# Gated cross attention and a block-sparse feed forward on one core: the feed forward's transposes leave TensorE

## The chip, the cores and the metric

One core of a Trainium2 chip runs the whole kernel. The metric is the device time of one launch in microseconds. Lower is better. Three runs of the kernel before gave 1849.33, 1851.08 and 1852.5 us; their median is 1851.08 us.

## What is computed

The reference is one layer: cross attention with a gate, then a feed forward that keeps one inner value of each block of 32, also with a gate. Both are preceded by a layer norm.

```python
x = x + tanh(g_xattn[0]) * xattn(layernorm(x), ctx, mask, bias, Wq, Wk, Wv, Wo)   # x: (32, 64, 512), 32 heads of 128
x = x + tanh(g_ffn[0]) * ffn(layernorm(x), c1_w, c2_w, w1, w2t)

def ffn(x):                                   # xf: (2048, 512) rows
    inter = xf @ c1_w.T @ c2_w.T              # rank 16, then 1792 inner values
    blk = inter.reshape(B * T, 56, 32)
    idx = argmax(blk, axis=-1) + arange(0, 1792, 32)   # the first largest of each block
    h = relu(einsum('bkm,bm->bk', w1[idx], xf))
    return einsum('bk,bkm->bm', h, w2t[idx])
```

The kernel doesn't gather rows. It computes all 1792 values of `xf @ w1.T`, multiplies them by a mask that is one at the first largest of each block, and multiplies the result by `w2t`. Everything is in fp32. A large product is made of three matmuls on a high and a low part of each operand (`three`, L1487 to L1490).

## The kernel before

The 2048 rows are 16 tiles of 128 rows (`PAIRS`). There are three stages. The first projects q, k and v and stores them in device memory. The second is attention: 128 slots (`SLOTS`, 16 groups of heads by 8 tiles), taken in 64 pairs (`DUOS`, loop variable `d`). The third is the feed forward over the 16 tiles. No scheduler places anything: each engine's program is written out, and semaphores join them. The order in a queue is the order of the code, and an instruction that waits holds everything behind it on its engine. This holds for SyncE as well, which issues all DMAs of these stages.

Per tile `t` the feed forward does this:

- VectorE norms the tile (`f_stats`, `f_norm`; GpSimd makes the reciprocal root in `do_rstd`), TensorE turns it by four transposes (`f_transpose_x`), ScalarE copies the high part (`fx_hi`) and VectorE takes the low part (`fx_lo`).
- TensorE `low_rank(u)` makes the rank-16 product for two tiles at once (12 matmuls of 256 columns), VectorE `low_rank` splits it, and TensorE `selector(t, k)` makes the 1792 selector values in four pieces.
- ScalarE copies these (`sel`), VectorE takes the maximum of each block (`block_max`) and marks the equal ones (`mark_max`, tile `is_max`), GpSimd multiplies the marks by a falling weight (`rank`), and VectorE finds the first (`block_rank`, `first_max`).
- TensorE `hidden(t, k)` makes `xf @ w1.T` in pieces of 512, 512, 512 and 256 columns, 12 matmuls each. VectorE `pick_h` takes the relu and the mask (tile `h_picked`).
- TensorE turns `h_picked` by 14 transposes (`transpose_h`), ScalarE copies the high part (`ht_hi`), VectorE takes the low part (`ht_lo`), TensorE makes 42 matmuls of 512 columns (`output`), and VectorE adds the gated result to the tile (`finish`). SyncE stores it.

In the main loop, iteration `j` on TensorE holds `output(j - 1)`, the transposes of `h_picked` of tile j between its pieces, and `hidden(j + 1)` with `selector(j + 2)` piece by piece. VectorE's iteration `j` holds the low parts of tile j, `block_rank`, `first_max` and `pick_h` of tile j + 1, and `block_max` and `mark_max` of tile j + 2. The weights w1 and w2 are split during attention into high and low parts, stored in device memory, and loaded back from slot 120 on (`load_w1`, `load_w2`, seven pieces of 1 MB each). PSUM has eight banks; `ffn_uses` lists which use of the feed forward has which bank, and `bank_free` gives the semaphore that frees it.

## Time and profile before

| | us |
|---|---|
| median of three runs | 1851.08 |
| the profiled execution | 1849.7 |
| its span, first to last instruction | 1847.5 |
| TensorE busy in the span | 1833.6 (99%) |
| VectorE, ScalarE, GpSimd busy | 1089.4, 686.3, 955.5 |
| share of the end chain on TensorE | 79% |

The span is the time between the first and the last instruction of one execution. Busy time of TensorE counts overlapping matmuls once. A matmul row of 512 columns has a duration of 0.39 us, but the next one starts 0.23 us after it, so the step between starts is what a matmul costs here. In the rows below, "idle before" is the idle time of an engine just ahead of a group, with the instruction that ended it. The projections take until about 940 us, attention until about 1482 us, and the feed forward the rest.

### The profile page before, as it was taken

To read this page: it belongs to the slowest core of one execution; us is meant where nothing else is said; L and a number is where in the kernel's file an instruction comes from. 1 tells how busy PE (TensorE), PEld (TensorE's weight loads), DVE (VectorE), ACT (ScalarE), POOL (GpSimd) and SP (SyncE) were. 2 spreads that over 40 slices of the span, in tenths; PEclk is the share of its full clock that TensorE was granted. 3 is DMA by queue.
4 is the path that set the end of the run, shared out by engine and by line. 5 is a ranking of instruction groups with operands and counts; after the bars stand their busy time and mean duration, and the time that the engine had idled before them with its cause. 6 is when DMAs were issued, how large, how long until landed. Compare 5 with 4: busy or idle time off the path is not lost.

```text
span 1847.5 us, 37822 instructions
## 1 busy us (share of the span) xinstructions
PE 1833.6 (99%) x15260; PEld 1580.0 (86%) x15260; DVE 1089.4 (59%) x1774; ACT 686.3 (37%) x1761; POOL 955.5 (52%) x758
## 2 busy tenths in 40 slices
PE   9999999999999999999999999999999999999999
PEld 7899988899998888888878888888888888888887
DVE  5444467433346465333457676786676887777673
ACT  4322233322233233333346556555555422222221
POOL 5767688766668888778735334333333121111110
PEclk9999999999999999999999999999999999999999
DMA  5555566644455554467658878798787650000000
GB/s 183 198 173 185 192 203 201 211 143 161 142 188 189 183 186 165 165 219 244 230 206 359 339 277 319 301 377 347 274 328 292 249 200 25 26 25 23 24 12 18
DMA packets 131293, 359.51 MB, mean 195 GB/s; under 512 B 12080, under 2 KB 53424, under 8 KB 120624
## 3 DMA queue, kind: packets, MB, share of 16 engines
q1 hardware_dynamic: 131120, 357.09, 53.9%
q8 instruction: 122, 2.00, 0.4%
q14 instruction: 51, 0.42, 0.1%
HBM read 229.11 MB, written 127.93 MB: 193 GB/s over the span
## 4 chain that ended last, share of the span: by engine, by line
PE 79%; DVE 2%; DMA 1%; ACT 1%; issue 1%; POOL 0%; DVEq 0%; SPq 0%; ACTq 0%
PE bank L1488 23%; PE bank L1490 22%; PE bank L1489 22%; PE bank L1589 3%; PE bank L1553 3%; PE bank L1569 2%; PE bank L1702 1%; PE bank L1679 1%; DMA x_tile<-in_x 1%; ACT scores L891 0%; PE bank L1658 0%; DMA ln_x<-in_x 0%; DVE attn_sum L1296 0%; DVE attn_t_lo L1268 0%; POOL wv_s_lo L751 0%
## 5 line engine op out<-in xcount | busy, mean ns | idle before, releaser
L1488 PE MATMUL bank<-tokens_hi,wkq_hi 128*128 128x512 f32 x888 | 346.8, 391 | 1.5 <-DVE tokens_lo L1063 0.8
L1489 PE MATMUL bank<-tokens_lo,wkq_hi 128*128 128x512 f32 x888 | 345.7, 389 | 0.0
L1490 PE MATMUL bank<-tokens_hi,wkq_lo 128*128 128x512 f32 x888 | 345.5, 389 | 0.0
L751 POOL TENSOR_TENSOR wkq_lo<-raw_wkq,wkq_hi 128x768 fp32r<-128x768 f32 x126 | 278.6, 2232 | 122.3 <-ACT wkq_hi L856 122.3
L1488 PE MATMUL bank<-wv_s_hi,tokens_hi 128*128 128x256 f32 x896 | 253.8, 283 | 1.5 <-POOL wv_s_lo L751 1.5
L1490 PE MATMUL bank<-wv_s_hi,tokens_lo 128*128 128x256 f32 x896 | 253.6, 283 | 0.0
L1489 PE MATMUL bank<-wv_s_lo,tokens_hi 128*128 128x256 f32 x896 | 253.6, 283 | 0.0
L1488 PE MATMUL bank<-wo_hi,attn_t_hi 128*128 128x512 f32 x512 | 205.7, 402 | 1.2 <-DVE attn_t_lo L1268 1.2
L1488 PEld LDWEIGHTS bank<-tokens_hi,wkq_hi 128*128 128x128 f32 x888 | 166.7, 188 | 39.3 <-DVE c L1113 3.0
L1490 PE MATMUL bank<-wo_hi,attn_t_lo 128*128 128x512 f32 x512 | 199.8, 390 | 0.0
L1489 PE MATMUL bank<-wo_lo,attn_t_hi 128*128 128x512 f32 x512 | 199.3, 389 | 0.0
L1490 PEld LDWEIGHTS bank<-tokens_hi,wkq_lo 128*128 128x128 f32 x888 | 166.7, 188 | 34.8
L1489 PEld LDWEIGHTS bank<-tokens_lo,wkq_hi 128*128 128x128 f32 x888 | 166.8, 188 | 33.8
L891 ACT ACTIVATE scores<-scores,negmax 128x64 f32<-128x64 f32 x512 | 172.2, 337 | 44.7 <-DVE negmax L1178 44.7
L880 ACT ACTIVATE p<-bank 128x512 f32<-128x512 f32 x94 | 56.2, 598 | 334.2 <-PE bank L1490 334.2
L751 POOL TENSOR_TENSOR wv_s_lo<-raw_wv,wv_s_hi 128x1536 fp32r<-128x1536 f32 (+1 forms) x32 | 130.1, 4065 | 96.1 <-ACT wv_s_hi L856 96.1
L1091 DVE TENSOR_TENSOR c<-bank,u 128x512 f32<-128x512 f32 x94 | 65.0, 692 | 188.2 <-PE bank L1490 188.2
L1488 PEld LDWEIGHTS bank<-wv_s_hi,tokens_hi 128*128 128x128 f32 x896 | 172.0, 192 | 2.5 <-POOL wv_s_lo L751 2.4
L1489 PEld LDWEIGHTS bank<-wv_s_lo,tokens_hi 128*128 128x128 f32 x896 | 172.0, 192 | 0.2
L1490 PEld LDWEIGHTS bank<-wv_s_hi,tokens_lo 128*128 128x128 f32 x896 | 172.0, 192 | 0.0
L779 POOL TENSOR_TENSOR wo_lo<-raw,wo_hi 128x1024 fp32r<-128x1024 f32 x30 | 71.6, 2388 | 158.0 <-DVE wo_hi L1255 158.0
L1113 DVE TENSOR_TENSOR c<-bank,u 128x512 f32<-128x512 f32 x94 | 64.7, 688 | 148.1 <-PE bank L1490 148.0
(148 smaller groups left out, 3688.4 us busy)
## 6 DMA issues: line engine op xcount, KB each, us to landing
k_t<-c SPq DMA_DIRECT2D x128, 256.0 KB, 2.4
v_by_token<-c SPq DMA_DIRECT2D x128, 256.0 KB, 2.3
q_t<-c SPq DMA_DIRECT2D x128, 256.0 KB, 2.3
kt<-k_t SPq DMA_DIRECT2D x16, 2048.0 KB, 9.7
qt<-q_t SPq DMA_DIRECT2D x16, 2048.0 KB, 14.2
v<-v_by_token SPq DMA_DIRECT2D x16, 2048.0 KB, 12.8
raw_wkq<-in_wk SPq DMA_DIRECT2D x32, 512.0 KB, 4.1
raw_wv<-in_wv SPq DMA_DIRECT2D x16, 1024.0 KB, 5.4
```

Of the source, the lines that this page charges most:

```text
L751: pool.tensor_tensor(lo, job_raw(r)[:, a:b, :], hi.bitcast(F32), ALU.subtract)\
L779: pool.tensor_tensor(lo, raw[n % 2][:, 0:cols], hi.bitcast(F32), ALU.subtract)\
L880: act.activation(e1[n % 2][:, :], bank[n % 2][:, :], ACT.Copy).then_inc(act_e1, 1)
L891: e = act.activation(sc[s % 2][:, h, :], sc[s % 2][:, h, :], ACT.Exp, bias=negmax[s % 2][:, h:h + 1], scale=1.0, accum_out=rsum[s % 2][:, ...
L1091: dve.tensor_tensor(o_c["c12"][n % 2][:, :], bank[5 + n % 2][:, :], u2[:, :], ALU.add)\
L1113: dve.tensor_tensor(o_c["c22"][n % 2][:, :], bank[5 + n % 2][:, :], u3[:, :], ALU.add)\
L1488: pe.matmul(o, a[0], b[0], start=first_mm, stop=False, skip_group_check=not grouped)
L1489: pe.matmul(o, a[0], b[1], start=False, stop=False, skip_group_check=not grouped)
L1490: return pe.matmul(o, a[1], b[0], start=False, stop=last_mm, skip_group_check=not grouped)
L1553: mm = pe.matmul(bank[SCORE_BANK[r % 2]][h * S:(h + 1) * S, o:o + S], qt[it % 2][:, 2 * r_ + h, cols], kt[it % 2][:, 2 * r_ + h, cols], st ...
L1569: mm = pe.transpose(bank[PT_BANK[d % 2]][:, o:o + P], sc[a][:, 2 * r:2 * r + 2, :].rearrange("p h k -> p (h k)"), ident[:, :])
L1589: mm = pe.matmul(bank[PV_BANK[b]][dims, o:o + S], v[it % 2][keys, p, h, dims], pt[keys, s % 2, h, :], start=True, stop=True)
```

## The change

The transposes of the feed forward leave TensorE. VectorE turns a tile in blocks of 32 by 32 (`transpose` in `f_norm` and in the new `turn_h`), the result is stored to device memory, and loaded back so that the rows of each block land where the full transpose needs them (`store_xf`, `load_xf`, `store_h`, `load_h` on SyncE). The order of the inner dimension in c1, w1 and w2 is permuted to suit (`by_block`). ScalarE reads the high parts from SBUF, and GpSimd takes over both low parts (`fx_lo`, `ht_lo`) from VectorE. `h_picked` is turned in two halves, of 1024 and of 768 columns (`HALF`).

The rank-16 product holds high and low parts of c1 in one stationary tile, so it is 8 matmuls of 256 columns and not 12. `hidden` and the selectors run one tile further ahead: iteration `j` has `output(j - 1)`, `hidden(j + 2)` and `selector(j + 3)`. Six tiles (`X_EARLY`) are normed and turned in attention, one per pair of slots from d = 56 on, where before two were normed at d = 60 and two at its end. w2's fourth piece is asked for in attention, and its pieces 5 and 6 ahead of 4. The tiles have nine buffers (`X2R`), and the arena grows from 207 to 222 KB.

```diff
 def ffn_uses():
...
+    sel, hid = (2, 3), (4, 5, 1, 6, 0)
...
@@ sync @@
+            def store_xf(t):
+                sp.wait_ge(dve_xb, t + 1)
+                sp.dma_start(xf_d[t], fxb[t % 2][:, :]).then_inc(xf_out[t % 2], 16)
+            def load_xf(t):
+                sp.wait_ge(xf_out[t % 2], 16 * (t // 2 + 1))
...
+            def store_h(t, i):
+                sp.wait_ge(dve_hb, 2 * t + i + 1)
+                sp.dma_start(h_d[i][t], hmb[i][:, :]).then_inc(h_out[i], 16)
+            def load_h(t, i):
+                sp.wait_ge(h_out[i], 16 * (t + 1))
+                if t:
+                    sp.wait_ge(pool_hl, 4 * (t - 1) + 2 * i + 2)
+                sp.dma_start(hraw[i][:, :, :], h_d[i][t].rearrange("(q g) (r f) -> (g r) q f", q=4, r=4))\
+                    .then_inc(h_in[i], 16)
...
@@ gpsimd @@
+            def ht_lo(t, g):
+                pool.wait_ge(act_h, 4 * t + g + 1)
+                pool.tensor_tensor(hmt_part(g, 1), hraw_part(g), hmt_part(g, 0).bitcast(F32), ALU.subtract)\
+                    .then_inc(pool_hl, 1)
...
+            for j in range(-1, PAIRS):
+                if j >= 0:
+                    for g in range(4):
+                        ht_lo(j, g)
+                if j % 2 == 0 and j + 7 < PAIRS:
+                    do_rstd(LN + j + 6)
+                    do_rstd(LN + j + 7)
+                if j + 3 < PAIRS:
+                    rank(j + 3)
+                if j % 2 and j + 6 < PAIRS:
+                    fx_lo(j + 5)
+                    fx_lo(j + 6)
@@ vector @@
+                    dve.transpose(fxb[t % 2][:, :], fxn[:, :]).then_inc(dve_xb, 1)
...
+            def turn_h(t, i):
+                a, w = HALF[i]
+                dve.wait_ge(dve_hm, 4 * t + 2 * i + 2)
+                if t:
+                    dve.wait_ge(h_out[i], 16 * t)
...
+                dve.transpose(hmb[i][:, :], hm[:, a:a + w]).then_inc(dve_hb, 1)
...
+            for j in range(-1, PAIRS + 1):
+                if j < 0:
+                    low_rank(1)
+                if j % 2 and 0 < j and j + 6 < PAIRS:
+                    f_norm((j + 5, j + 6))
+                if j + 2 < PAIRS:
+                    block_rank(j + 2)
+                    first_max(j + 2)
+                if j > 0:
+                    finish(j - 1)
+                if j % 2 and 0 < j and j + 3 < PAIRS:
+                    low_rank((j + 3) // 2)
+                for k in range(4):
+                    if j + 2 < PAIRS:
+                        pick_h(j + 2, k)
+                        if k % 2:
+                            turn_h(j + 2, k // 2)
+                    if j + 3 < PAIRS:
+                        block_max(j + 3, k)
+                    if k == 2 and j % 2 == 0 and j + 7 < PAIRS:
+                        f_stats((j + 6, j + 7))
+                if j + 3 < PAIRS:
+                    mark_max(j + 3)
@@ tensor @@
-            def f_transpose_x(t):
...
-            def transpose_h(t, k):
...
+            for j in range(1, PAIRS + 1):
                 for k in range(4):
                     output(j - 1, k)
+                    if j == 1:
+                        selector(3, k)
+                if j % 2 and j + 3 < PAIRS:
+                    low_rank((j + 3) // 2)
                 for k in range(4):
+                    if j + 2 < PAIRS:
+                        hidden(j + 2, k)
+                    if j + 3 < PAIRS:
+                        selector(j + 3, k)
```

GpSimd at the start of the feed forward, before: the marks of two tiles (`rank(0)`, `rank(1)`) after the statistics of tiles 2 and 3, and then more of the same (`is_max` is the tile of marks).

```order
L762 TENSOR_TENSOR ln_rstd_61<-ln_var_eps_59,minus_half 128x1 [waits pool_own]
L784 TENSOR_TENSOR is_max<-is_max,earlier_is_larger 128x1792 [waits dve_ffn_ismax] x2
L758 TENSOR_SCALAR ln_var_eps_58<-ln_mean_var_56 128x1 [waits dve_xn,dve_stat]
L762 TENSOR_TENSOR ln_rstd_60<-ln_var_eps_58,minus_half 128x1 [waits pool_own]
L758 TENSOR_SCALAR ln_var_eps_59<-ln_mean_var_57 128x1 [waits dve_xn,dve_stat]
```

GpSimd at the same place, now (the `xft_lo` rows are `fx_lo`, the `h_picked_t_lo` rows `ht_lo` of tile 0).

```order
L880 TENSOR_TENSOR is_max<-is_max,earlier_is_larger 128x1792 [waits dve_ffn_ismax]
L870 TENSOR_TENSOR xft_lo<-raw_xft_184,xft_hi 128x4x128 [waits act_ffn_xt_hi]
L870 TENSOR_TENSOR xft_lo<-raw_xft_185,xft_hi 128x4x128 [waits act_ffn_xt_hi]
L880 TENSOR_TENSOR is_max<-is_max,earlier_is_larger 128x1792 [waits dve_ffn_ismax] x2
L870 TENSOR_TENSOR xft_lo<-raw_xft_184,xft_hi 128x4x128 [waits act_ffn_xt_hi]
L870 TENSOR_TENSOR xft_lo<-raw_xft_185,xft_hi 128x4x128 [waits act_ffn_xt_hi]
L875 TENSOR_TENSOR h_picked_t_lo<-raw_h_t_188,h_picked_t_hi 128x512 [waits act_ffn_ht_hi] x2
L875 TENSOR_TENSOR h_picked_t_lo<-raw_h_t_189,h_picked_t_hi 128x512 [waits act_ffn_ht_hi]
```

The low parts of tile 0, which `output(0)` needs, stand on GpSimd behind the marks of tiles 1 and 2 and the low parts of x of tiles 4 and 5.

VectorE before, from `mark_max(3)` at the end of iteration 1 to the split of the rank-16 product of tiles 4 and 5 in iteration 2.

```order
L1347 TENSOR_TENSOR is_max<-selector,block_max 128x1792 [waits dve_ffn_first,dve_step]
L1377 TENSOR_TENSOR h_picked_t_lo<-bank,h_picked_t_hi 128x512 [waits act_ffn_ht_hi] x2
L1316 TENSOR_TENSOR xft_lo<-bank,xft_hi 128x4x128 [waits act_ffn_xt_hi] x2
L1352 TENSOR_REDUCE block_first<-is_max 128x56 [waits pool_ffn_rank]
L1377 TENSOR_TENSOR h_picked_t_lo<-bank,h_picked_t_hi 128x512 [waits act_ffn_ht_hi]
L1358 TENSOR_TENSOR first_max_155<-is_max,block_first 128x1792 [waits dve_ffn_hm,dve_step]
L1377 TENSOR_TENSOR h_picked_t_lo<-bank,h_picked_t_hi 128x256 [waits act_ffn_ht_hi]
L1328 CAST low_rank_stacked_182<-bank 128x256 [waits pe_ffn_inter,pe_ffn_t]
L1330 TENSOR_TENSOR low_rank_stacked_182<-bank,low_rank_stacked_182 64x256 [waits dve_step]
```

VectorE now, from `mark_max(3)` to the same split for tiles 4 and 5 (iteration 1).

```order
L1448 TENSOR_TENSOR is_max<-selector,block_max 128x1792 [waits dve_ffn_first,dve_step]
L1181 TENSOR_SCALAR xn<-x_tile_178,ln_mean_var_56,ln_rstd_60 128x512 [waits pool_rstd,dve_ffn_xn_by_block]
L1420 STREAM_TRANSPOSE xn_by_block_182<-xn 128x512 [waits dma_ffn_xn_by_block0,dve_xn]
L1181 TENSOR_SCALAR xn<-x_tile_179,ln_mean_var_57,ln_rstd_61 128x512 [waits pool_rstd,dve_ffn_xn_by_block]
L1420 STREAM_TRANSPOSE xn_by_block_183<-xn 128x512 [waits dma_ffn_xn_by_block1,dve_xn]
L1453 TENSOR_REDUCE block_first<-is_max 128x56 [waits pool_ffn_rank]
L1459 TENSOR_TENSOR first_max_155<-is_max,block_first 128x1792 [waits dve_ffn_hm,dve_step]
L1486 SCALAR_TENSOR_TENSOR x_tile_172<-bank,gate_tanh,x_tile_172 128x512 [waits pe_ffn_out]
L1429 CAST low_rank_stacked_192<-bank 128x256 [waits pe_ffn_inter,pe_ffn_t]
L1431 TENSOR_TENSOR low_rank_stacked_192<-bank,low_rank_stacked_192 64x256 [waits dve_step]
```

The split of the rank-16 product now stands behind the marks of tile 3, GpSimd's work on them, the two operations that find the first, and the finish of tile 0.

TensorE before, where the rank-16 product of tiles 4 and 5 begins (behind the transposes of `h_picked` of tile 2; the selectors of tile 3 were done one iteration earlier).

```order
L1702 MATMUL bank<-ident,h_picked 128x128 [waits dve_ffn_hm,dve_ffn_xt_lo]
L1702 MATMUL bank<-ident,h_picked 128x128
L1488 MATMUL bank<-xft_hi,c_hi 128x256 [waits dve_ffn_xt_lo]
L1489 MATMUL bank<-xft_lo,c_hi 128x256
L1490 MATMUL bank<-xft_hi,c_lo 128x256
```

TensorE now, from the last selector piece of tile 3 to the first matmuls of `hidden(3, 0)`; `selector(4, 0)`, which waits for the split (`dve_ffn_t`), comes 12 matmuls after the first of these.

```order
L1757 MATMUL bank<-c_stacked,low_rank_stacked_193 128x256 [waits dve_ffn_t,act_ffn_inter]
L1746 MATMUL bank<-xft_hi,c_stacked 128x256 [waits pool_ffn_xt_lo,act_ffn_inter]
L1746 MATMUL bank<-xft_hi,c_stacked 128x256 x3
L1746 MATMUL bank<-xft_lo,c_stacked 128x256 x4
L1573 MATMUL bank<-w_hi,xft_hi 128x512 [waits pool_ffn_xt_lo,dve_ffn_hm]
```

So between the selector piece of tile 3 that VectorE's marks need and the selector piece of tile 4 that needs VectorE's split there are 8 matmuls of 256 columns and 12 of 512.

## Rows read from the trace of the kernel before

**Rows 1.** The page, part 1: busy time, share of the span, instructions.
```profile
PE 1833.6 (99%) x15260; PEld 1580.0 (86%) x15260; DVE 1089.4 (59%) x1774; ACT 686.3 (37%) x1761; POOL 955.5 (52%) x758
```

**Rows 2.** Waits of TensorE from 1440 us to the end: total, times, longest.
```profile
PE bank L1488 <- DVE h_picked L1368: 0.7, 1, 0.7
```

**Rows 3.** TensorE in order of time: start, duration, instruction, feed forward.
```profile
1622.40 0.39 PE L1489 MATMUL bank<-w_lo,h_picked_t_hi 128*128 128x512 f32 x1
...
1622.86 0.60 PE L1702 MATMUL bank<-ident,h_picked 128*128 128x128 f32 x4
1623.21 0.47 PE L1488 MATMUL bank<-w_hi,h_picked_t_hi 128*128 128x512 f32 x1
1623.52 0.39 PE L1489 MATMUL bank<-w_lo,h_picked_t_hi 128*128 128x512 f32 x1
...
1626.48 1.18 PE L1658 MATMUL bank<-ident,xn 128*128 128x128 f32 x8
1627.41 0.47 PE L1488 MATMUL bank<-w_hi,h_picked_t_hi 128*128 128x512 f32 x1
...
1632.06 0.38 PE L1702 MATMUL bank<-ident,h_picked 128*128 128x128 f32 x2
1632.19 0.36 PE L1488 MATMUL bank<-xft_hi,c_hi 128*128 128x256 f32 x1
...
1633.70 0.40 PE L1488 MATMUL bank<-w_hi,xft_hi 128*128 128x512 f32 x1
...
1646.88 0.60 PE L1702 MATMUL bank<-ident,h_picked 128*128 128x128 f32 x4
```

**Rows 4.** TensorE in order of time, end of attention.
```profile
1481.91 1.03 PE L1658 MATMUL bank<-ident,xn 128*128 128x128 f32 x8
```

**Rows 5.** VectorE groups, 1550 to 1750 us: busy, mean ns, idle before.
```profile
L1347 DVE TENSOR_TENSOR is_max<-selector,block_max 128x1792 bf16<-128x1792 f32 x9 | 18.2, 2026 | 0.3
L1358 DVE TENSOR_TENSOR first_max<-is_max,block_first 128x1792 bf16<-128x1792 bf16 x9 | 18.1, 2015 | 0.0
L1368 DVE SCALAR_TENSOR_TENSOR h_picked<-bank,first_max 128x512 f32<-128x512 f32 x26 | 18.0, 692 | 23.8 <-PE bank L1490 23.1
L1070 DVE BATCH_NORM_STATS2 ln_stats<-x_tile 128x6 f32<-128x512 f32 x8 | 5.5, 689 | 0.0
L1330 DVE TENSOR_TENSOR low_rank_stacked<-bank,low_rank_stacked 64x256 fp32r<-64x256 f32 x4 | 1.7, 428 | 0.1
```

**Rows 6.** VectorE groups of the whole span, one form each.
```profile
L1083 DVE STREAM_TRANSPOSE ln_xn_by_block<-ln_xn 128x512 f32<-128x512 f32 x16 | 11.2, 701 | 0.0
L1076 DVE TENSOR_SCALAR xn<-x_tile,ln_mean_var,ln_rstd 128x512 f32<-128x512 f32 x16 | 8.6, 545 | 4.5 <-POOL ln_rstd L762 4.5
L1063 DVE TENSOR_TENSOR tokens_lo<-raw_tokens,tokens_hi 128x1024 fp32r<-128x1024 f32 x19 | 32.2, 1693 | 7.0 <-ACT tokens_hi L873 7.0
L1063 DVE TENSOR_TENSOR tokens_lo<-raw_tokens_first,tokens_hi 128x1024 fp32r<-128x1024 f32 x3 | 3.7, 1221 | 0.4 <-ACT tokens_hi L873 0.4
```

**Rows 7.** VectorE in order of time, first tiles of the feed forward.
```profile
1490.73 2.03 DVE L1347 TENSOR_TENSOR is_max<-selector,block_max 128x1792 bf16<-128x1792 f32 x1
1492.67 2.21 DVE L1368 SCALAR_TENSOR_TENSOR h_picked<-bank,first_max 128x512 f32<-128x512 f32 x4
```

**Rows 8.** GpSimd in order of time.
```profile
1452.70 1.27 POOL L779 TENSOR_TENSOR c_lo<-raw,c_hi 128x512 fp32r<-128x512 f32 x1 [12.34 <-ACT c_hi L955]
1492.84 3.60 POOL L784 TENSOR_TENSOR is_max<-is_max,earlier_is_larger 128x1792 bf16<-128x1792 bf16 x1 [8.60 <-DVE is_max L1347]
```

**Rows 9.** Start of the kernel, windows of 1 us: length, TensorE busy (instructions), clock, DMA.
```profile
3.00:4.00 1.00, 1.00 (x6) 1.00 1.02 381
5.00:6.00 1.00, 1.00 (x9) 1.00 0.84 279
7.00:8.00 1.00, 1.00 (x12) 1.00 0.93 328
```

**Rows 10.** DMA issues, 1525 to 1840 us: count, size, us to landing.
```profile
out<-x_tile SPq DMA_DIRECT2D x14, 256.0 KB, 2.0
```

More of the change, by code:

```diff
@@ L92, in ffn_uses @@
 def ffn_uses():
[L94 to L118 removed]
+    used = {}
@@ new lines, in next_of @@
+    def next_of(banks, use):
+        k = used.get(banks, 0)
+        used[banks] = k + 1
+        return (use, banks[k % len(banks)])
+    sel, hid = (2, 3), (4, 5, 1, 6, 0)
+    out = [(("t", 0), 0), (("sel", 0, 0), 7), (("sel", 0, 1), 0)]
+    out += [next_of(sel, ("sel", 0, k)) for k in (2, 3)]
+    out += [next_of(sel, ("sel", 1, k)) for k in (0, 1)]
+    out += [next_of(hid, ("h", 0, k)) for k in (0, 1)]
+    out += [next_of(sel, ("sel", 1, k)) for k in (2, 3)]
+    out += [next_of(hid, ("h", 0, k)) for k in (2, 3)]
@@ new lines, in ffn_uses @@
+    out.append(next_of(sel, ("t", 1)))
+    out += [next_of(hid, ("h", 1, 0)), (("h", 1, 1), 7), next_of(sel, ("sel", 2, 0))]
+    for k in (2, 3):
+        out += [next_of(hid, ("h", 1, k)), next_of(sel, ("sel", 2, k - 1))]
+    out += [next_of(hid, ("h", 2, 0)), next_of(sel, ("sel", 2, 3))]
+    out += [next_of(hid, ("h", 2, k)) for k in (1, 2, 3)]
+    for j in range(1, PAIRS + 1):
+        out.append(next_of(hid, ("out", j - 1)) if j == PAIRS - 1 else (("out", j - 1), 7))
+        if j == 1:
+            out += [next_of(sel, ("sel", 3, k)) for k in range(4)]
+        if j % 2 and j + 3 < PAIRS:
+            out.append(next_of(sel, ("t", (j + 3) // 2)))
+        for k in range(4):
@@ L688, in _ @@
                         load_w1(n)
-                if s == SLOTS - 6:
-                    load_x2(3)
+                for t in range(X_EARLY):
+                    if s == SLOTS - 22 + 2 * t:
+                        load_x2(t)
+                    if s == SLOTS - 14 + 2 * t:
+                        store_xf(t)
+                    if t < 4 and s == SLOTS - 11 + t + t // 2 * 5:
+                        load_xf(t)
                 if it % G == G - 1 and it < ITERS:
@@ L697, in _ @@
                     sp.wait_ge(kept_out, 32 * KEPT)
[L698 to L710 removed]
+                for n in {0: (0,), 1: (1, 2, 3)}.get(s - SLOTS, ()):
+                    load_w2(n)
+            load_w2(5)
+            load_w2(6)
+            load_w2(4)
+            load_xf(4)
+            load_xf(5)
+            store_h(0, 0)
+            for j in range(-1, PAIRS + 1):
+                ahead = j % 2 and 0 < j and j + 6 < PAIRS
+                if j + 1 < PAIRS:
+                    store_h(j + 1, 1)
+                if ahead:
+                    store_xf(j + 5)
+                    store_xf(j + 6)
+                if j < 0:
+                    load_h(0, 0)
+                    load_h(0, 1)
+                    load_x2(6)
+                    load_x2(7)
+                    load_x2(8)
+                if X2R <= j + 7 < PAIRS:
+                    load_x2(j + 7)
+                if 0 <= j < PAIRS - 1:
+                    load_h(j + 1, 0)
+                if ahead:
+                    load_xf(j + 5)
+                    load_xf(j + 6)
+                if 0 <= j < PAIRS - 1:
+                    load_h(j + 1, 1)
+                if j > 0:
+                    sp.wait_ge(dve_o, j)
+                    sp.dma_start(out[j - 1], x2[(j - 1) % X2R][:, :]).then_inc(out_sem[(j - 1) % X2R], 16)
+                if j + 2 < PAIRS:
+                    store_h(j + 2, 0)
             for k in range(X2R):
@@ L830, in _ @@
                         do_lo(n)
-            for j in range(PAIRS):
-                if j % 2 and j + 4 < PAIRS:
-                    do_rstd(LN + j + 3)
-                    do_rstd(LN + j + 4)
-                if j + 2 < PAIRS:
-                    rank(j + 2)
+            for j in range(-1, PAIRS):
[10 more added lines that the diff above has]
+                    fx_lo(j + 6)
         @block.scalar
```

334 lines of the change are left out of this document (137 added, 197 removed).

## The prediction

> **What bounds the kernel now.** I read the page's busy times first: TensorE is busy for 99% of the span, no other engine for more than 59% [rows 1]. Then the waits of TensorE from the end of attention on: one, of 0.7 us [rows 2]. So the feed forward is TensorE's own queue, end to end, and an instruction taken out of it is worth its step as long as nothing becomes late. Third, TensorE in order of time, for the steps [rows 3]: from 1622.40 to 1622.86 there are two steps, so matmuls of 512 columns start 0.23 us apart, whatever their listed duration of 0.39.
>
> **What leaves TensorE.** Four transposes take from 1622.86 to 1623.21, and the matmul behind them takes a step of 0.31 instead of 0.23: 0.43 us. Two take 0.13 and cost the next matmul 0.09: 0.22. A tile has three groups of four and one of two, 1.51 us; 16 tiles give 24.2. Eight transposes of x, from 1626.48 to 1627.41, with the longer step behind them, are 1.01 for two tiles, 8.1 for all. The rank-16 product, 12 matmuls from 1632.19 to 1633.70, has a step of 0.12, and loses four of them eight times: 3.8. Sum: **36.1 us less** on TensorE [rows 3]. Its iteration was 24.0 us with such a product in it (1622.86 to 1646.88); it becomes 21.1, and 20.1 without.
>
> **What VectorE and GpSimd get.** VectorE loses both low parts (about 3 us a tile) and gains transposes: 0.70 for 512 columns [rows 6], so by length about 1.2 and 0.9 for the halves. Listed durations of neighbours overlap: four picks take 2.21 together [rows 7]. A tile costs it 2.2 for the picks, 2.2 for the block maxima, which are as long, 2.03 + 2.0 + 2.0 for marks and first, 0.75 for the finish (one PSUM and one SBUF input like a pick), 2.1 for the halves, and on average 2.6 for norm, turn, statistics and split [rows 5, 6]: 15.9 of 20.6 us. GpSimd: 3.6 for the marks, a low part of 512 columns at 1.27 [rows 8], four pieces of h 4.5, x 1.3: about 10. Nobody is full. The trips through memory (a store lands in 2.0 us [rows 10]; I give a load 2.5) have two iterations of room in the steady loop. The cost is in the order of the queues, at three places.
>
> **Before output(0).** Attention's matmuls ended at 1481.9 [rows 4]; without the x transposes and four matmuls ahead of it, at about 1480.4. From there TensorE has hidden of three tiles (9.6 each), the selectors and one rank-16 product, 30.9 us, and wants output(0) at 1511.4. That needs the low part of h, which GpSimd makes behind rank(2) and two low parts of x. The chain to it: mark_max(1) began at 1490.73 [rows 7], and begins 1.2 earlier, since GpSimd's first marks follow TensorE: done 1491.5. VectorE then picks and turns tile 0 (4.4), splits (0.85), finds the first of tile 1 (4.0), picks and turns tile 1 with tile 2's maxima (6.9), and marks tile 2 (2.0): 1509.6. GpSimd: marks 3.6, x twice 2.5, h 1.3: 1517.2 with the gaps between engines [rows 5, 8]. **A wait of 5.7 us.** The trips of h hide behind this chain: the store can go at 1496, has 3 MB of w2 ahead of it, 8 us at the 381 GB/s of a full queue [rows 9], and with its own 2.0 and the load's 2.5 the data are there at 1508.5, 7 us ahead of need. Another wait I take at selector(0): TensorE comes 1.5 earlier by what was removed ahead of it, VectorE's split does not have to. Bounds 0 and 1.5, value 0.8.
>
> **In iteration 1.** The selectors of tile 3 are placed between the pieces of output(0), so they end with it, and not at the end of an iteration. Behind them TensorE has 1.0 of rank-16 and 2.7 of hidden(3, 0), and then selector(4, 0), which waits for VectorE's split of tiles 4 and 5. VectorE gets to it by way of the last copies and picks of tile 2 and its turn, which lag 3.1 (the statistics of two tiles, 1.75, stand there), mark_max(3) 2.0, GpSimd's marks 3.7, block_rank and first_max 4.0, finish 0.75, split 0.9, and gaps: about 14.7 after the selectors, against 3.7 [rows 3, 5, 8]. **A wait of 11.0 us.** It happens once; afterwards selectors end with the iteration.
>
> **In the odd iterations 3, 5, 7, 9.** Counted from the iteration's start, VectorE marks by 5.2 (it had two statistics in the even one), GpSimd by 8.9 (the norms and turns of two tiles, 2.6, run meanwhile), first found 13.0, finish 13.7, split 14.7. TensorE is at that selector at 13.3. **1.4 us each, 5.6.** In 11 and 13 there are no norms, and no wait by this count. For the even ones no split is waited for.
>
> **The clock after a wait.** TensorE never waits over 2.4 us in this trace, so no row shows what a wait of 5 or 11 us does. The start of the kernel is the nearest: the same matmul is done 6 times in a microsecond at 3 us, 9 times at 5 us and 12 times at 7 us [rows 9], so for about 3 us the rate is that of the lower level, 1.2 GHz and not 2.4, a loss of 1.5 us, though the granted clock in the rows reads 1.00 there. Bounds: 0, and 1.5 at each of the two long waits and each of the four short ones, 9. I take two, 3.1, since the long ones are nearest to a start.
> The Trainium skill (TensorE: Matmul & The Clock Gate, "Loop structure matters more than you think") says that a long wait between matmuls drops TensorE to the low clock. The half rate at the start agrees with its rule for an idle engine; no run here shows it in the middle. By it the sum has the 3.1, without it 3.1 less.
>
> **Two engines in SBUF.** A VectorE subtraction with two SBUF inputs took 1.22 us where GpSimd was quiet and 1.69 among GpSimd's work [rows 6]. Now GpSimd works while VectorE is in first_max. Bounds: 0, and 0.8 at each of the five waits that first_max is part of, 4.0. I take a third, 1.4, because GpSimd is busy in the feed forward for half of the time only.
> The Trainium skill (GPSIMD Engine Reference, "Specifications") has the rule: GpSimd shares its SBUF interfaces with VectorE, with contention where VectorE reads two SBUF inputs or runs in a two-port mode. The two rows agree, and the rule speaks against this change: by it the sum has the whole 4.0.
>
> **In attention** VectorE gets 2.0 us more per pair of slots from d = 55 to 61. It idles for 41% of the span [rows 1], and the new work stands at the end of its turns, ahead of a step that waits for TensorE; I take nothing, and 2 us as the other bound. The same goes for SyncE, whose new stores wait for the turns: the weights behind them come up to 4 us later, and the last piece of w1 is not asked for later than before.
>
> **Sum.** −36.1 + 5.7 + 0.8 + 11.0 + 5.6 + 3.1 + 1.4 = −8.5. The profiled execution took 1849.7 us (span 1847.5 and 2.2 around it), so 1841.2; the median shown is 1.4 above it, so **1842.6**.
>
> **Rivals.**
> 1. The waits at output(0) and selector(4, 0) come, but neither a clock loss nor contention, and the odd iterations just fit: −36.1 + 17.5 = −18.6, so 1832.5. For it: 1.4 of 13.3 us is little, and VectorE's steps overlap by 0.09. Against: the rows at the start and the pair of subtractions.
> 2. Nothing waits: the whole 36.1, 1815. It would need GpSimd's marks off the way to output(0), and the order rows say they are on it.
> 3. Slower: VectorE and GpSimd hold the loop. Each tile has 15.9 of VectorE and, in the even iterations with nothing to fill it, 3.7 of waiting for GpSimd's marks: 19.6, against 20.6 of TensorE on average. If the factor of the two subtractions, 1.69/1.22, holds for the marks, for first_max and for GpSimd's marks in every tile, that is 0.8 + 0.8 + 1.4 = 3.0 more, 22.6, and TensorE waits 2.0 in each of 13 iterations: 26.0. They take the place of the 5.6 and 1.4: −8.5 − 7.0 + 26.0 = +10.5, so 1861.6. It decides from 20.6 us of chain per tile. For it: the pair of rows. Against: marks and first_max run while GpSimd mostly waits for VectorE.
> 4. The trips of h are late at the start, where the queue is full: if the data come at 1521 instead of 1508.5, output(0) waits 5 us longer: −3.5, so 1847.6. For it: 7 MB of w2 and the last stores of x stand in the same queue. Against: 7 us of room.
>
> **Chances.** Forecast 0.50 (its own range 1836 to 1848), rival 1 0.28, rival 2 0.05, rival 3 0.09, rival 4 0.08. Against the median, 0.2% is 3.7 us, about what a measurement of this kernel can tell from no change. Below 1847.4: all of 1 and 2, nine tenths of the forecast and a third of rival 4: 0.81. Within: 0.10. Slower: 0.09. The range leaves out rival 2 and most of 3: 1829 to 1851.
>
> **What would show it.** In the trace of the changed kernel: TensorE waits once, 5 to 6 us, for GpSimd's h_picked_t_lo near 1511; once, about 11, for VectorE's split behind the selectors of tile 3; and a little over 1 us four times for the same split. TensorE's busy time falls by some 36 us. The matmuls behind the two long waits start 0.45 us apart for about 3 us. VectorE's first_max stays between 2.0 and 2.8. If the first long wait is for a DMA, rival 4 holds; if TensorE waits in every iteration, rival 3; if iteration 1 has no wait, my reading of the queues is wrong.

## The result, and the profile after

The changed kernel takes 1860.6 us (median of 4 runs, 1858.7 to 1863.4), the kernel before 1851.0 beside it (1849.3 to 1852.5): ratio 1.0054, 95% interval 1.0036 to 1.0071. It is slower by half a per cent; I had said 1842.6 and faster. The profiled execution took 1858.7 (span 1856.9), 17.5 us more than the 1841.2 that my sum gave for it.

The page of the changed kernel, busy times and TensorE's granted clock over 40 slices of the span:

```profile
PE 1803.4 (97%) x14940; PEld 1552.0 (84%) x14940; DVE 1102.8 (59%) x1742; ACT 688.2 (37%) x1761; POOL 1073.3 (58%) x838
...
PEclk9999999999999999999999999999999988999999
```

TensorE is busy for 30.2 us less than before [rows 1], with 320 matmuls fewer, and yet the span grew by 9.4. So it now stands still for 39.6 us that it did not before, and two slices show less than the full clock. Of the 39.6 us, 38.8 are in the waits of the next two lines, so the tiles that are normed and turned in attention cost TensorE next to nothing there. Waits of TensorE from 1380 us to the end (total, times, longest), where before there was one of 0.7 [rows 2]:

```profile
PE bank L1757 <- DVE low_rank_stacked L1431: 28.8, 7, 12.8
PE bank L1573 <- DVE h_picked L1469: 10.7, 1, 10.7
```

The same in order of time, the instruction that each wait of over 1 us ends with (start, duration, instruction, idle time before; three more of 3.33 or 3.34 follow at 1645.89, 1690.36 and 1734.81):

```profile
1468.59 1.05 PE L1757 MATMUL bank<-c_stacked,low_rank_stacked 128*128 128x512 f32 x4 [1.41 <-DVE low_rank_stacked L1431]
...
1499.87 0.47 PE L1757 MATMUL bank<-c_stacked,low_rank_stacked 128*128 128x512 f32 x1 [1.20 <-DVE low_rank_stacked L1431]
...
1525.46 0.76 PE L1573 MATMUL bank<-w_hi,h_picked_t_hi 128*128 128x512 f32 x1 [10.73 <-DVE h_picked L1469]
...
1555.41 0.77 PE L1757 MATMUL bank<-c_stacked,low_rank_stacked 128*128 128x512 f32 x1 [12.82 <-DVE low_rank_stacked L1431]
...
1601.43 0.47 PE L1757 MATMUL bank<-c_stacked,low_rank_stacked 128*128 128x512 f32 x1 [3.33 <-DVE low_rank_stacked L1431]
```

The places are those that the prediction named: output(0), the first selector behind those of tile 3, and the selectors of the odd iterations. The sizes are not. The releaser named at 1525.46 is misleading: VectorE's pick there has nothing to do with output(0); what output(0) needs is GpSimd's first low part of h, which ends at 1525.36. First wait, GpSimd; the third row holds all four low parts, the fourth row the first of them alone, and VectorE's first_max stands beside it:

```profile
1516.36 3.56 POOL L880 TENSOR_TENSOR is_max<-is_max,earlier_is_larger 128x1792 bf16<-128x1792 bf16 x1 [18.10 <-DVE is_max L1448]
1519.88 2.48 POOL L870 TENSOR_TENSOR xft_lo<-raw_xft,xft_hi 128x512 fp32r<-128x512 f32 x2
1522.32 6.18 POOL L875 TENSOR_TENSOR h_picked_t_lo<-raw_h_t,h_picked_t_hi 128x512 fp32r<-128x512 f32 x4
...
1522.32 3.04 POOL L875 TENSOR_TENSOR h_picked_t_lo<-raw_h_t,h_picked_t_hi 128x512 fp32r<-128x512 f32 x1
```

```profile
1522.01 2.23 DVE L1459 TENSOR_TENSOR first_max<-is_max,block_first 128x1792 bf16<-128x1792 bf16 x1
```

Marks, two low parts of x, then h: the order that the prediction had, but the marks begin at 1516.36, not 1509.6. Why is in VectorE's row of the same stretch, and in SyncE's DMA issues:

```profile
1509.57 1.25 DVE L1482 STREAM_TRANSPOSE h_by_block<-h_picked 128x1024 f32<-128x1024 f32 x1 [3.76 <-DMA h_by_block<-h_by_block]
```

```profile
1498.52 0.32 SPq L613 DMA_DIRECT2D w_hi<-w_hi_lo  x1
1498.89 0.43 SPq L613 DMA_DIRECT2D w_lo<-w_hi_lo  x1
1499.42 0.92 SPq L646 DMA_DIRECT2D raw_xft<-ffn_xn_by_block  x2
1500.40 2.52 SPq L651 DMA_DIRECT2D h_by_block<-h_by_block  x2
1509.49 1.31 SPq L657 DMA_DIRECT2D raw_h_t<-h_by_block  x2
```

VectorE's turn of tile 1 writes the buffer out of which tile 0 is stored. The store is issued at 1500.40 behind w2; SyncE's load, which waits for it to land, goes at 1509.49, and VectorE, which waits for the same, at 1509.57, after 3.76 us. The third wait is VectorE's queue in iteration 1:

```profile
1542.17 2.02 DVE L1448 TENSOR_TENSOR is_max<-selector,block_max 128x1792 bf16<-128x1792 f32 x1
1544.12 0.54 DVE L1181 TENSOR_SCALAR xn<-x_tile,ln_mean_var,ln_rstd 128x512 f32<-128x512 f32 x1
1544.69 0.71 DVE L1420 STREAM_TRANSPOSE xn_by_block<-xn 128x512 f32<-128x512 f32 x1
1545.44 2.93 DVE L1181 TENSOR_SCALAR xn<-x_tile,ln_mean_var,ln_rstd 128x512 f32<-128x512 f32 x1
1548.40 0.71 DVE L1420 STREAM_TRANSPOSE xn_by_block<-xn 128x512 f32<-128x512 f32 x1
1549.03 1.98 DVE L1453 TENSOR_REDUCE block_first<-is_max 128x56 bf16<-128x1792 bf16 x1
1551.04 2.76 DVE L1459 TENSOR_TENSOR first_max<-is_max,block_first 128x1792 bf16<-128x1792 bf16 x1
1553.73 0.74 DVE L1486 SCALAR_TENSOR_TENSOR x_tile<-bank,gate_tanh,x_tile 128x512 f32<-128x512 f32 x1
1554.39 0.41 DVE L1429 CAST low_rank_stacked<-bank 128x256 fp32r<-128x256 f32 x1
```

with GpSimd's marks beside it:

```profile
1544.28 3.80 POOL L880 TENSOR_TENSOR is_max<-is_max,earlier_is_larger 128x1792 bf16<-128x1792 bf16 x1 [2.86 <-DVE is_max L1448]
```

The same norm takes 0.54 and then 2.93 us. The long one ends at 1548.37, and GpSimd's marks at 1548.08. This repeats in each odd iteration up to 9, ten norms in all (count, then busy, mean ns, idle before):

```profile
L1181 DVE TENSOR_SCALAR xn<-x_tile,ln_mean_var,ln_rstd 128x512 f32<-128x512 f32 x10 | 17.5, 1754 | 0.2
```

Their mean of 1.75 is against 0.55 before [rows 6]. And first_max takes 2.76, against 2.02 [rows 5].

Last, the clock behind the waits. Windows of 1 us: length, TensorE busy (instructions), clock, DMA share and GB/s:

```profile
1526.00:1527.00 1.00, 1.00 (x4) 0.50 0.00 0
1530.00:1531.00 1.00, 1.00 (x4) 0.50 0.72 167
1532.00:1533.00 1.00, 1.00 (x6) 1.00 0.00 1
1556.00:1557.00 1.00, 1.00 (x4) 0.50 0.73 182
1560.00:1561.00 1.00, 1.00 (x6) 1.00 0.00 0
1737.00:1738.00 1.00, 1.00 (x4) 0.50 0.51 195
```

Granted clock 0.50 is the lower level, 1.2 GHz, and matmuls start 0.43 us apart, not 0.23: 14 of them from 1525.46 (2.9 us lost), 8 from 1555.41 (1.65), about 7 near 1736 to 1739, behind a wait of 3.33 (1.5).

### The profile page after: what moved, and what is told of

Its sections match the earlier page's. It is cut to its first block, busy times and chain, and to the rows that moved or that the text cites. A ratio compares the mean times of both kernels' runs of the same rounds, so it can differ in the third digit from the quotient of the medians.

```text
span 1856.9 us, 37340 instructions
## 1 busy us (share of the span) xinstructions
PE 1803.4 (97%) x14940; PEld 1552.0 (84%) x14940; DVE 1102.8 (59%) x1742; ACT 688.2 (37%) x1761; POOL 1073.3 (58%) x838
## 4 chain that ended last, share of the span: by engine, by line
PE 70%; DVE 6%; issue 4%; POOL 1%; DMA 1%; ACT 1%; DVEq 0%; ACTq 0%; POOLq 0%
PE bank L1573 21%; PE bank L1575 20%; PE bank L1574 20%; PE bank L1674 3%; PE bank L1638 3%; PE bank L1654 2%; DVE xn L1181 1%; DMA x_tile<-in_x 1%; DVE block_first L1453 1%; POOL is_max L880 1%; PE bank L1757 1%; DVE attn_sum L1401 1%; ACT scores L996 1%; DVE ln_stats L1175 0%; DVE is_max L1448 0%
## 5 line engine op out<-in xcount | busy, mean ns | idle before, releaser
L1573 PEld LDWEIGHTS bank<-tokens_hi,wkq_hi 128*128 128x128 f32 x888 | 166.7, 188 | 38.8 <-DVE c L1218 3.0
```

What stands on the lines that cost most here:

```text
L1573: pe.matmul(o, a[0], b[0], start=first_mm, stop=False, skip_group_check=not grouped)
```

## The experiments

All are edits of the changed kernel, timed in 3 to 5 rounds beside the kernel before, whose median in these calls was 1850.3, 1850.4 and 1850.0. They ask which wait each step of a queue makes, what the long norm is, and what the half rate is worth.

**1. GpSimd's order at the start** (lo_first).

```
+            for g in range(4):
+                ht_lo(0, g)
             for j in range(-1, PAIRS):
-                if j >= 0:
+                if j >= 1:
                     for g in range(4):
                         ht_lo(j, g)
```

> The changed kernel with one edit: GpSimd makes the low parts of h of tile 0 ahead of the marks of tile 2 and the low parts of x of tiles 4 and 5. Theory (the order of GpSimd's queue holds output(0)): ScalarE has the high part of h at 1513.9, so the first low part is done near 1515.3 and TensorE's wait of 10.73 us there falls to under 1 us, its half-rate stretch with it. The marks of tile 2 start some 2 us later (4.5 us of h from 1513.9 against 1516.36), first_max(2) ends near 1526.4, and from there VectorE has 11 us of its own work up to the end of mark_max(3): 1537.4 instead of 1544.2. The split of tiles 4 and 5 comes 6.8 earlier, while TensorE is there 13 us earlier: its wait of 12.8 grows to about 19, and the whole kernel gains 6.8: about 1854. Rival (the wait is for the DMA, h itself late): the 10.73 stays at 8 or more and the time within 2 us of 1860.6. Second rival (the second wait is VectorE work that moves along with TensorE): gain 13, 1848.

Measured: 1857.1 us (1853.3 to 1859.6), ratio 1.0036 (1.0024 to 1.0049). TensorE at output(0) and behind the selectors of tile 3, and GpSimd:

```profile
1517.79 0.47 PE L1575 MATMUL bank<-w_hi,h_picked_t_hi 128*128 128x512 f32 x1 [1.61 <-issue]
...
1552.20 0.76 PE L1759 MATMUL bank<-c_stacked,low_rank_stacked 128*128 128x512 f32 x1 [19.39 <-DVE low_rank_stacked L1433]
```

```profile
1516.42 6.24 POOL L875 TENSOR_TENSOR h_picked_t_lo<-raw_h_t,h_picked_t_hi 128x512 fp32r<-128x512 f32 x4 [16.70 <-ACT h_picked_t_hi L1086]
1522.62 3.61 POOL L880 TENSOR_TENSOR is_max<-is_max,earlier_is_larger 128x1792 bf16<-128x1792 bf16 x1
```

The first wait goes from 10.73 to 1.61, so nearly all of it was GpSimd's order and not the data; the next grows from 12.8 to 19.4, as expected (19). The two waits are one chain through VectorE: the first gives 9.1 and the second takes 6.6 of it back. The gain is 3.5 and not 6.8, because the four low parts took 6.2 us and began at 1516.42, so GpSimd's marks came 4 us later than expected; the half rate stands behind two of the four waits of 3.33.

**2. VectorE's split earlier** (split_first).

```
+                if j == 1:
+                    low_rank(2)
                 if j % 2 and 0 < j and j + 6 < PAIRS:
                     f_norm((j + 5, j + 6))
                 if j + 2 < PAIRS:
                     block_rank(j + 2)
+                if j % 2 and 1 < j and j + 3 < PAIRS:
+                    low_rank((j + 3) // 2)
+                if j + 2 < PAIRS:
                     first_max(j + 2)
                 if j > 0:
                     finish(j - 1)
-                if j % 2 and 0 < j and j + 3 < PAIRS:
-                    low_rank((j + 3) // 2)
```

> The changed kernel with one edit: VectorE splits the rank-16 product of tiles 4 and 5 ahead of the norms of iteration 1, and in the iterations 3, 5, 7, 9 right behind block_rank, ahead of first_max and finish. Theory (TensorE waits for the split's place in VectorE's queue): the wait of 12.8 falls by the 10.2 us between the end of mark_max(3) and the split's old start, to 2.6; the four of 3.33 lose first_max 2.7 and finish 0.7 and vanish; the half-rate stretches behind them (1.65 and 1.5 us) go too. Sum 10.2 + 13.3 + 3.1 = 26.6: about 1834. Rival (VectorE and GpSimd hold the loop with what contention adds): the waits come back for picks or low parts of h further on, and the gain is less than half: 1848 or more.

Measured: **1834.5 us** (1833.6 to 1835.6), ratio 0.9914 (0.990 to 0.9927). Moving two VectorE instructions, the split, turns the change from slower to faster. TensorE: the wait is 2.56 (2.6 expected), one of 2.34 for finish(0) is new, and of the four of 3.33 one of 1.75 is left. Windows of 50 us of the same kernel:

```profile
1600.00:1650.00 50.00, 50.00 (x238) 1.00 0.41 129
1650.00:1700.00 50.00, 50.00 (x243) 1.00 0.42 133
```

From 1600 on TensorE does not wait, though the norms of the odd iterations still take 2.97 there. So VectorE and GpSimd do not hold the loop, contention and all; rival 3 of the prediction is out, and that its time, 1861.6, was nearest is luck.

**3. The first trip of h ahead of w2** (h_first).

```
-            load_w2(5)
-            load_w2(6)
-            load_w2(4)
             load_xf(4)
-            load_xf(5)
             store_h(0, 0)
+            load_xf(5)
...
                     load_h(0, 1)
+                    load_w2(5)
+                    load_w2(6)
+                    load_w2(4)
```

> The changed kernel with one edit: SyncE issues the first store of h and both loads of it ahead of the last three pieces of w2. Theory (the first trip of h waits in the DMA queue behind 3 MB of w2): VectorE's wait of 3.76 us for the block buffer goes, the marks of tile 2 start near 1512.6 instead of 1516.36, TensorE's wait of 10.73 falls to 7.0, and everything behind moves along: about 1857. Rival (the trip is as long whatever stands ahead of it): no change, 1860.6. Second rival (now w2 is late): TensorE waits for a DMA in output(0), and the gain is lost.

Measured: 1858.9 us (1857.0 to 1859.7), ratio 1.0044 (1.0031 to 1.0056). The turn of tile 1 no longer waits (it starts at 1506.62), and the wait at output(0) is 7.03, as expected:

```profile
1522.53 0.77 PE L1573 MATMUL bank<-w_hi,h_picked_t_hi 128*128 128x512 f32 x1 [7.03 <-DVE h_picked L1469]
```

Of the 3.7 only 1.7 show in the time. In the profiled execution the half rate now stands behind three of the four waits of 3.33, where in the changed kernel it was one; at some 1.5 us each that is the missing 2 and more.

**4. Unused matmuls in the waits** (filler: the two long ones; fill_all: the four of 3.33 too). `fill(o, n)` issues n matmuls of 512 columns into the bank that is used next, and nothing reads what they leave.

```
+                if t in (4, 6, 8, 10, 12) and k == 0:
+                    fill(bank[f_bank[("sel", t, k)]], 54 if t == 4 else 13)
                 pe.wait_ge(dve_ft, u + 1)
...
+                if t == 0 and k == 0:
+                    fill(bank[f_bank[("out", t)]], 45)
                 pe.wait_ge(pool_hl, 4 * t + k + 1)
```

> The changed kernel with matmuls whose results are not used added in the two long waits of TensorE: 45 of 512 columns (10.3 us at 0.23) ahead of output(0), 54 (12.4 us) ahead of the first selector of tile 4. Theory (the half rate comes from the idleness): the granted clock stays at 1.00, the matmuls behind both places start 0.23 us apart at once, which is worth 2.9 + 1.65 us: about 1856. Rival (the clock drops for another reason, or the fillers push the chain): no gain or slower, 1860.6 or more.

> The kernel with the unused matmuls of the filler run, and 13 more of 512 columns (3.0 us) in each of the four waits of 3.33 ahead of the first selectors of tiles 6, 8, 10 and 12. Theory (any wait of 3 us or more can bring the half rate, and in the filler run it came behind short waits in place of the long ones): the granted clock is 1.00 throughout the feed forward, all six half-rate microseconds of the changed kernel (2.9 + 1.65 + 1.5) are gone, about 1854.6. Rival (the half rate comes at times of its own, whatever TensorE does): stretches under 1.00 stay, and the time is that of the filler run, 1857.6, or more.

Measured: filler 1857.6 us (1855.0 to 1861.5), ratio 1.0040 (1.0027 to 1.0052); fill_all 1853.0 (1851.5 to 1854.7, 11 runs), ratio 1.0016 (1.0007 to 1.0025). In filler the clock behind both long waits is 1.00, but all four waits of 3.33, of which one had it in the changed kernel, now have the half rate behind them, as here:

```profile
1598.79 0.77 PE L1763 MATMUL bank<-c_stacked,low_rank_stacked 128*128 128x512 f32 x1 [3.32 <-DVE low_rank_stacked L1431]
```

In fill_all no window in which TensorE works is below 1.00, and the kernel is 7.6 us faster (7.0 by the two ratios) with 151 matmuls more and the same chain on VectorE:

```profile
1599.00:1600.00 1.00, 1.00 (x6) 1.00 0.30 110
1736.00:1737.00 1.00, 1.00 (x11) 1.00 0.98 401
```

So the half rate comes from TensorE's idleness, and cost 6 to 8 us here: 6.1 by the steps, 7.6 by this run.

**5. What the long norm is** (norm_apart, dve_rank, quarters). Three edits: the norms moved out of the marks' time; the ranks made on VectorE; GpSimd's marks in four instructions.

```
norm_apart:
+                if j % 2 == 0 and 0 <= j and j + 7 < PAIRS:
+                    f_norm((j + 6, j + 7))
                 if j + 3 < PAIRS:
                     mark_max(j + 3)
dve_rank (block_rank, ahead of its reduce; rank(t) leaves GpSimd):
-                dve.wait_ge(pool_e, t + 1)
+                dve.wait_ge(dve_e, t + 1)
+                after(link(dve.tensor_tensor(is_max[:, :, :], is_max[:, :, :],
+                    rank_w[:, :].unsqueeze(1).broadcast_to([P, NBLK, SPARSITY]), ALU.mult)))
quarters (rank(t) on GpSimd):
+                for q in range(4):
+                    part = is_max[:, 14 * q:14 * (q + 1), :]
```

> The changed kernel with one edit: VectorE norms and turns the two coming tiles at the end of the even iteration, ahead of mark_max, instead of at the start of the odd one, where GpSimd makes its marks. Theory (VectorE's norm and GpSimd's marks get in each other's way): every norm takes 0.55 us, none 2.9. The chain to the split gets 2.6 longer by the moved work and 1.1 shorter behind it (from the end of mark_max to block_rank 3.75 instead of 4.83), so the waits of 12.8 and 3.33 become about 14 and 4.8 and the time rises by some 7 us, 1868. Rival (the second norm is long by its own form or by its place behind a transpose): it stays at 2.9 where it is now.

> The changed kernel with one edit: the product of is_max with the ranks is made by VectorE ahead of block_rank and not by GpSimd; nothing else moves. Theory (contention with GpSimd's marks): the norms take 0.55 us each and first_max 2.03, since GpSimd is idle or at small work beside them. From the end of mark_max to the split: norms and turns 2.5, ranks 2.0, block_rank 2.0, first_max 2.0, finish and split 1.6, 10.1 us instead of 11.2, so the waits of 12.8 and 3.33 become 11.7 and 2.2, five times 1.1: about 1855. Rival (VectorE's 2.0 us more per tile hold the loop): TensorE waits in even iterations too, and the kernel is slower than 1861. Second rival (no contention, the long norm is its own): the norm stays at 2.9 and the waits at 3.3 or more.

> The changed kernel with one edit: GpSimd makes the ranks of a tile in four instructions of 448 columns instead of one of 1792. Theory (VectorE's norm and an instruction of GpSimd exclude each other: the norm runs when the one on GpSimd has ended): the second norm of an odd iteration, 2.9 us beside one instruction, ends behind the quarter that it meets, in 1.5 us or less, while GpSimd's marks take 3.7 plus at most 1 in all; block_rank starts when they end. The waits of 3.33 fall by 0.8 at most if the quarters cost nothing, and rise by as much as the four cost more: 1858 to 1862. Rival (both slow down by sharing, whatever the length of GpSimd's instruction): the second norm stays near 2.9.

Measured, the norms of the feed forward in norm_apart, dve_rank and quarters, each group's columns being busy, mean ns and idle before:

```profile
L1181 DVE TENSOR_SCALAR xn<-x_tile,ln_mean_var,ln_rstd 128x512 f32<-128x512 f32 x10 | 5.4, 540 | 0.2
```

```profile
L1175 DVE TENSOR_SCALAR xn<-x_tile,ln_mean_var,ln_rstd 128x512 f32<-128x512 f32 x10 | 10.8, 1079 | 0.2
```

```profile
L1182 DVE TENSOR_SCALAR xn<-x_tile,ln_mean_var,ln_rstd 128x512 f32<-128x512 f32 x10 | 9.7, 970 | 0.2
```

norm_apart: all norms at 0.54, so the 2.9 is GpSimd's work beside them and nothing in the norm. Time 1871.8 (1870.2 to 1873.7), ratio 1.0111 (1.0095 to 1.0127), above the 1868 expected: the waits are 13.55 and 4.02, near the 14 and 4.8 expected, but the half rate stands behind every one of them, mean clock 0.984. quarters: 1857.1 (1855.8 to 1857.7), ratio 1.0039 (1.0024 to 1.0053); the second norm and the quarters:

```profile
1546.35 1.38 DVE L1182 TENSOR_SCALAR xn<-x_tile,ln_mean_var,ln_rstd 128x512 f32<-128x512 f32 x1
```

```profile
1545.19 4.41 POOL L882 TENSOR_TENSOR is_max<-is_max,earlier_is_larger 128x448 bf16<-128x448 bf16 x4 [2.85 <-DVE is_max L1449]
```

A shorter instruction on GpSimd makes a shorter norm on VectorE, 1.38 for 2.93. So says exclusion, by which an instruction ends only behind the one that it met on the other engine; sharing, by which both are slow for as long as they overlap, does not. The waits fall from 12.82 to 12.02 and from 3.33 to about 2.5. That is the 0.8 which I had given if the quarters cost nothing, but they cost 0.6 (4.41 for 3.80), and the time is just below my 1858 to 1862. Only 0.3 comes from the norm, since block_rank starts 4.5 us after mark_max and not 4.8; the rest is first_max, 2.23 for 2.76, which met less of a low part of h, and that I had not foreseen.

dve_rank: 1845.5 us (1844.2 to 1848.2), ratio 0.9974 (0.9963 to 0.9985), 10 better than I expected. I had forgotten that this edit too takes the marks from in front of h on GpSimd: at output(0) TensorE does not wait (first matmul at 1515.23), and the next waits are 14.2 and 2.30. The norm is 1.5 us at the first of a pair and 0.6 at the second: GpSimd is then at its low parts of h. The ranks cost VectorE 1.05 us where GpSimd is quiet, against 3.56 to 3.80 for GpSimd in the changed kernel.

**6. Together** (best: edits 1 and 3, the split of tiles 4 and 5 and finish(0) in iteration 0, later splits behind block_rank; best_dve_rank: and the ranks on VectorE; best2: and this).

```
+                if j == 2:
+                    finish(1)
+                if j == 3:
+                    low_rank(3)
+                    finish(2)
                 if j + 2 < PAIRS:
                     block_rank(j + 2)
```

> The changed kernel with all three orders changed: GpSimd's low parts of h of tile 0 first, the first trip of h ahead of w2, and VectorE's split of tiles 4 and 5 inside iteration 0 (behind the maxima of tile 3's second block), finish of tile 0 at the end of iteration 0, the later splits behind block_rank. Theory: the wait at output(0) goes (10.7, and 2.9 of half rate), so does the one behind the selectors of tile 3 (12.8 and 1.65), the four of 3.33 fall to under 1 on average (13.3 less some 3), and a half-rate stretch of 1.5: about 1821. The removed 36.1 us of TensorE work would then show nearly whole: 1851 - 36 + 2.6 of waits ahead of output(0) and a few us. Rival (a chain of VectorE and GpSimd of over 20 us per tile holds the loop once TensorE is not held up at the start): waits of 2 us or more in most iterations, and 1830 or more.

> The kernel of the run before this one, and VectorE makes the ranks itself. Theory (GpSimd's marks cost the chain 3.7 and contention): chain per tile shorter by 1.7 us in even and 1.1 in odd iterations, what waits were left in the loop go: 1 to 3 us faster than that kernel. Rival (VectorE's own 2 us per tile become the bound, 17.9 of 20.6 plus its waits for TensorE's products): slower by 2 us or more.

> The faster of the two reordered kernels (all orders changed, ranks on VectorE), with finish of tile 1 at the start of iteration 2 and the split of tiles 6 and 7 and finish of tile 2 at the start of iteration 3, behind the norms. Theory (what TensorE still waits for between 1555 and 1580, 2.0 us for finish and 3.0 for the split, is again the place in VectorE's queue): both go, with the half-rate stretch behind the second: 5 to 6 us less than 1824.5, about 1819. Rival (VectorE is behind by its own work there): the waits move to the picks behind them, 1823 or more.

Measured: best 1827.3 us (1826.9 to 1828.3), ratio 0.9874 (0.986 to 0.9888), 6 above expectation: TensorE still waits 1.4, 1.85, 1.6, 2.71, 2.08 and 2.33, two fifths of it for low parts of h that come late in iterations 1 and 2, and the half rate stands behind the 2.08. best_dve_rank 1824.5 (1823.8 to 1827.9), ratio 0.9862 (0.9848 to 0.9876), 2.8 less, within the 1 to 3 expected. best2 **1821.2** (1820.3 to 1822.6), ratio 0.9846 (0.9832 to 0.9860), faster than both kernels; 1819 was expected. Its page, busy times and clock:

```profile
PE 1796.9 (99%) x14940; PEld 1549.2 (85%) x14940; DVE 1117.9 (61%) x1758; ACT 687.3 (38%) x1761; POOL 1020.6 (56%) x822
...
PEclk9999999999999999999999999999999999999999
```

The wait for finish is gone; that for the split is not (3.07 at 1575.90). VectorE has no idle time from 1560.74 to the end of that split at 1575.76, and some 1.4 us of this is a mark_max of 2.40 and a norm of 1.51 beside GpSimd's low parts. So there VectorE is late by its own work, and half of the last theory failed.

## Why the prediction was wrong

**What leaves TensorE: right.** 36.1 forecast. With the clock at 1.00 throughout (best2) it is busy for 1796.9, 36.7 less than before [rows 1]. Where the changed kernel neither waits nor norms, its iterations are 19.9 us apart (finish at 1797.35 and 1817.28); 20.1 was forecast.

**Before output(0): right place, wrong size.** 5.7 forecast, 10.7 measured, and 1.2 more at 1499.87 for the split of tiles 2 and 3, which I had not priced. The step that failed is "the trips of h hide behind this chain". I followed the data of tile 0 to its user and did not ask who waits for the store to leave its buffer: the turn of tile 1 does, 3.76 us, and stands ahead of mark_max(2). Rival 4 had the late store (h at 1513.36 on ScalarE, its 1521 was too late), not this path. h_first showed it: with the trip ahead of w2 the wait fell by 3.7. The other 1.3 is the first low part of h, a term that I had at 1.3 us and that took 3.04: it started at 1522.32, behind the start of VectorE's first_max, which ended at 1524.24, and ended 1.1 us after it, about what such a low part takes alone (1.26). So here GpSimd waited for VectorE, a direction that the prediction had not priced. The marks of tile 2 and TensorE itself each came some 3 us later than forecast besides, which cancels in the wait.

**Selector(0):** 0.8 forecast, 1.41 measured. The half of my bounds was too kind: the wait is nearly the whole upper bound of 1.5, so the split hardly moved.

**In iteration 1 and in the odd iterations: the working was right, and the contention term under-sized.** 11.0 and 1.4 forecast, 12.82 and 3.33 measured: 1.8 and 1.9 more, at each of five places, 9.5 in all, where I had put 1.4 and had 4.0 as the far end. Each is first_max (0.7 to 0.8) and the long norm, 2.4 longer, of which 1.1 had no cover: block_rank starts 4.8 us after mark_max and not 3.7. I had let the norm run "meanwhile" at 0.55. Its factor is 5, and quarters shows that it is no factor at all but the rest of GpSimd's instruction. first_max is the same case: it began at 1551.04, met a low part of h that ended at 1551.92, and ended 1.9 us after that, nearly its usual 2.0.

The error was in the row that I took. The 1.69 of the pair of subtractions [rows 6] is the mean of 19, and in the trace of the kernel before 14 of them take 1.22 and four take 3.41 or 3.42. One of the four, and GpSimd's instruction that was running when it began:

```profile
602.56 3.42 DVE L1063 TENSOR_TENSOR tokens_lo<-raw_tokens,tokens_hi 128x1024 fp32r<-128x1024 f32 x1
```

```profile
602.05 2.85 POOL L751 TENSOR_TENSOR wkq_lo<-raw_wkq,wkq_hi 128x1024 fp32r<-128x1024 f32 x1
```

GpSimd's ends at 604.90 and VectorE's 1.08 us later. None of the 19 takes 1.69. So the second step that failed, and the larger one, is "1.69 among GpSimd's work", with the 0.8 at first_max alone that was taken from it: a mean over held and free instructions was read as a slowdown of each.
The Trainium skill (GPSIMD Engine Reference, "Specifications") names both cases, contention where VectorE has two SBUF inputs or is in a two-port mode. I quoted it and priced only the first. The norm has one tensor input, so of the two only the second could be its case; no run shows which mode it ran in.

**The clock: right cause, half the size.** 3.1 forecast, 6.1 read from the steps (2.9, 1.65 and 1.5), 7.6 from fill_all against the changed kernel. I had granted the half rate to the two long waits only, and 1.5 us to each; it lasted 6.1 us behind the first, and came behind one of 3.33 too. The Trainium skill (TensorE: Matmul & The Clock Gate, "Loop structure matters more than you think") says that a long wait between matmuls makes TensorE go cold. The trace agrees: the granted clock is 0.50 behind the waits of 10.73 and 12.82 us, in the middle of the kernel.

**Where the 17.5 us are:** waits ahead of and at output(0) 6.8 (5.0, 1.2 and 0.6), contention 9.5 less the 1.4 priced, 8.1, clock 3.0: 17.9 together, within half a microsecond of it. In attention I took nothing, which fits: outside the listed waits TensorE idles 0.8 us more than before. No single term made the sign. My -8.5 lay nearer to zero than the sum of what could go wrong in one direction: a wait's bound stops at nothing below, and adds up above. The chance of slower, 0.09, was tied to one rival alone, and not to several terms at their upper bounds at once.

**What stays open.** Why a wait of 3.33 is followed by the half rate in some iterations and runs and not in others was not settled; this may also be what scatters the times by a few us. Nor was the double buffer for h tried, or the change with its six early tiles taken out.

## What to carry to other kernels

When an edit takes work from the engine that is the bound, the next question is which instruction of the others stands ahead of what that engine wants: moving two VectorE instructions was worth 26 us here, beside the 36.7 us of TensorE work removed. For every store out of a single buffer, follow the next writer of the buffer too, and its queue. Before work is put beside a GpSimd instruction, look at single instructions of both engines and not at the mean of a group, ask which of them are held until the other's ends, and price waits with the clock that they cost behind them.
